# DLRM tower on one core: low parts in quarters between the one-hots, four lookups ahead of the second pair, transposes moved later

## The chip, the cores and the metric

One core of one Trainium2 chip runs the whole program. The metric is the device time in microseconds of one launch. Engines are named TensorE (PE), VectorE (DVE), ScalarE (ACT), GpSimd (POOL) and SyncE (SP).

## The reference

The batch has 2048 samples. Each has 26 ids, one into each of 26 tables of 128-wide fp32 rows, and a dense vector of 128 values. Eleven or twelve of the tables have only 1000 rows.

```python
e = stack([tbl_f[ids[:, f]] for f in range(26)], axis=1)   # (2048, 26, 128)
sd = einsum('bfd,bd->bf', e, dense)
pairs = einsum('bfd,bgd->bfg', e, e)[:, iu, ju]            # 325 pairs above the diagonal
z = concatenate([dense, sd, pairs], axis=1)
h = concatenate([z, dense], axis=1)                        # (2048, 607)
h = maximum(h @ W_top1 + b_top1, 0)                        # 512
h = maximum(h @ W_top2 + b_top2, 0)                        # 256
y = h @ W_top3
```

## The kernel before

The batch is cut into eight chunks of 256 samples, worked on in four pairs. The features of both chunks of a pair are collected in `feat`, transposed (128 values on the partitions). There are two ways into it.

**Lookups (l).** A small table is read by a matmul with one-hot columns. The table stays in SBUF as 125 partitions by 8 rows of 128, split into two parts that TensorE takes at its faster fp32r rate: a high part made by ScalarE (`split_hi`, step s) and a low part, the rest, made by VectorE (`split_lo`). ScalarE shifts the ids (`shift_ids`, i and j), VectorE makes the one-hots in four parts of two operations (`make_part`), three parts being held at a time (`PLACES`). TensorE's `lookup` takes each part with 4 matmuls, 16 in all, into one of two halves of `oh_ps`, and ScalarE copies the 512 columns to `feat` (`looked_up_to_feat`, c). The first pair has 12 lookups, the later ones 11; the tables are split during the first pair, their raw copies lying in eight buffers that later serve for other things.

**Gathers (r, q).** GpSimd gathers the rows of the other tables by indirect DMA, four DMAs for one unit, into a ring of six units. TensorE turns a unit with four transposes (`transposes`), ScalarE copies it out (`transposed_to_feat`). A q step turns a unit of the pair before. A unit's gathers wait for the transposes of the unit six before it.

**The rest.** `dot_products` (e for the pair's first chunk, d for the second, eight steps of 64 matmuls each) makes all pair products, which ScalarE and VectorE copy out and SP stores to DRAM and loads back in another layout (`store_products`, `make_z`). Layer 1 has four steps (k0 to k3, o0 to o3, m0 to m3) into `mlp_ps`, ScalarE adds the bias and cuts at zero; step 4 is layer 2; VectorE ends with `layer3`. Letters k, o and m mean chunks n-3, n-2 and n-1, with n the first chunk of the running pair.

The order of the steps is written out by hand in one list for each pair and one for the tail (`FIRST` to `TAIL`). TensorE and ScalarE both walk through these lists, each taking its own part of a step; VectorE and SP have loops of their own. Lines that the steps touch: `split_hi` L377, `shift_ids` L382, `transposed_to_feat` L391, `looked_up_to_feat` L399, `split_lo` L453, `make_part` L462, transposes L522, lookups L538, dot products L556, layer 1 L574, layer 2 L583, gathers L367, store of products L279, load of z L292 and L295.

A copy of a lookup may overwrite `feat` only when the dots of the pair before are done, and the dots need all copies of their chunk:

```python
if j:
    act.wait_ge(dots_done, 2 * j * GUNITS)          # looked_up_to_feat
...
if v == 0:                                          # dot_products
    pe.wait_ge(transposed_out, unit_no(n // 2, UNITS if n % 2 else ALONE + (n > 0)))
    pe.wait_ge(looked_up_out, looked(n // 2 + 1))
```

## Time and profile before

| what | value |
|---|---|
| median of 3 runs (lowest, highest) | 361.55 us (360.44, 361.7) |
| the profiled execution, its time | 359.05 us |
| its span, first to last instruction | 357.1 us |
| TensorE matmuls | 335.2 us busy, 94% |
| VectorE | 206.6 us, 58% |
| ScalarE | 204.0 us, 57% |
| GpSimd | 241.8 us, 68% |
| gathers, L367 | 236 DMAs, 1023 ns each |

The span leaves out what lies around the program, about 2 us. The profile is of one execution, so its durations are compared with its own time, and differences are then carried over to the median. Busy shares are means over stages with different limits; the rows further down are from single stages.

### The profile page before, as it was taken

Reading aid. Unit: us, or ns where it says so; the run is one execution under the profiler, and the core shown is the slowest. Engines: PE = TensorE matmul, PEld = TensorE weight load, DVE = VectorE, ACT = ScalarE, POOL = GpSimd, SP = SyncE. Lnnn points to the kernel's source line nnn. Section 1 sums busy time; section 2 is a strip of 40 time slices with the busy share of each in tenths; the row PEclk is TensorE's granted clock in tenths of the full one; section 3 lists DMA queues with packets and bytes.
Section 4 is the critical chain, followed back from the end, with each engine's and each line's share of the span. In section 5 each row is a group of like instructions: output and inputs, shape, how many; then the busy total and the mean of one; then the engine's idle time right before and its main releaser. Section 6 shows DMA issues by size and latency. Waiting matters only on the chain.

```text
span 357.1 us, 8260 instructions
## 1 busy us (share of the span) xinstructions
PE 335.2 (94%) x3388; PEld 286.4 (80%) x3388; DVE 206.6 (58%) x486; ACT 204.0 (57%) x267; POOL 241.8 (68%) x242
## 2 busy tenths in 40 slices
PE   0799999697999999999999999999999999999996
PEld 0677777586988888888998888898898888898885
DVE  0889898565328874628328886527427787145111
ACT  3378897484736575763663664872572666664111
POOL 6777777777777777777777777777777777720000
PEclk9999999999999999999999999999999999999999
DMA  6999729536355225254247243246236321124400
GB/s 154 241 261 250 194 61 269 148 93 164 76 143 138 65 69 132 55 127 124 53 108 183 75 105 84 68 95 155 59 83 177 100 64 48 51 51 121 113 24 1
DMA packets 46342, 40.93 MB, mean 115 GB/s; under 512 B 29039, under 2 KB 40423, under 8 KB 46306
## 3 DMA queue, kind: packets, MB, share of 16 engines
q1 hardware_dynamic: 38754, 24.94, 27.4%
q0 software_dynamic: 7552, 15.48, 17.3%
q8 instruction: 27, 0.44, 0.5%
q14 instruction: 9, 0.07, 0.1%
HBM read 34.64 MB, written 5.76 MB: 113 GB/s over the span
## 4 chain that ended last, share of the span: by engine, by line
PE 77%; POOL 8%; DMA 5%; issue 4%; DVE 3%; SPq 2%; ACT 1%; DVEq 0%
PE oh_ps L538 34%; PE dot_ps L556 15%; PE mlp_ps L574 15%; POOL rows L367 8%; PE mlp_ps L583 7%; PE tr_ps L522 7%; DMA rows<-tbl_dram,idx_sb 3%; DVE onehot L462 2%; DMA b_sb<-b_top_dram 2%; ACT feat L391 1%; DMA idx_sb<-idx_dram 0%; SPq L320 0%; SPq L316 0%; SPq L319 0%; DVE h L481 0%
## 5 line engine op out<-in xcount | busy, mean ns | idle before, releaser
L367 POOL DMA_INDIRECT rows<-tbl_dram,idx_sb x236 | 241.3, 1023 | 73.3 <-issue 70.7
L462 DVE TENSOR_SCALAR onehot<-ids_bc 125x512 fp32r<-125x512 int16 x360 | 142.4, 448 | 33.2 <-PE oh_ps L538 19.1
L538 PE MATMUL oh_ps<-onehot,table_hi 125*128 125x512 f32 x360 | 115.5, 402 | 12.0 <-DVE onehot L462 11.9
L538 PE MATMUL oh_ps<-onehot,table_lo 125*128 125x512 f32 x360 | 111.7, 392 | 0.0
L399 ACT ACTIVATE feat<-oh_ps 128x512 f32<-128x512 f32 x45 | 54.7, 1217 | 62.8 <-PE oh_ps L538 61.7
L391 ACT ACTIVATE feat<-tr_ps 128x512 f32<-128x512 f32 x59 | 73.0, 1241 | 26.3 <-PE tr_ps L522 25.8
L538 PEld LDWEIGHTS oh_ps<-onehot,table_hi 125*128 125x128 f32 x360 | 65.6, 190 | 24.4 <-issue 12.8
L538 PEld LDWEIGHTS oh_ps<-onehot,table_lo 125*128 125x128 f32 x360 | 68.1, 189 | 14.8
L556 PE MATMUL dot_ps<-feat 128*54 128x52 f32 x2048 | 57.8, 214 | 5.7 <-ACT feat L391 1.8
L556 PEld LDWEIGHTS dot_ps<-feat 128*54 128x54 f32 x2048 | 54.5, 130 | 10.1 <-issue 6.1
L471 DVE COPY dots<-dot_ps 54x416 f32<-54x416 f32 x56 | 33.2, 594 | 36.2 <-PE dot_ps L556 34.9
L574 PE MATMUL mlp_ps<-zt,w_sb 117*128 117x256 f32 x192 | 44.4, 380 | 0.0
L478 DVE TENSOR_TENSOR h<-mlp_ps,b_sb 128x256 f32<-128x256 f32 x16 | 6.8, 425 | 60.6 <-PE mlp_ps L583 60.6
L406 ACT ACTIVATE dots<-dot_ps 54x416 f32<-54x416 f32 x56 | 29.1, 522 | 18.3 <-PE dot_ps L556 15.6
L574 PEld LDWEIGHTS mlp_ps<-zt,w_sb 117*128 117x128 f32 x192 | 35.2, 190 | 4.3
L522 PE MATMUL tr_ps<-ident,rows 128*128 128x128 f32 x236 | 36.0, 275 | 1.2 <-DMA rows<-tbl_dram,idx_sb 1.2
L522 PEld LDWEIGHTS tr_ps<-ident,rows 128*128 128x128 f32 x236 | 28.1, 140 | 8.9 <-DMA rows<-tbl_dram,idx_sb 2.9
L382 ACT ACTIVATE ids_bc<-ids_bc,row_f 128x512 int16<-128x512 int16 x45 | 30.9, 701 | 3.6 <-DMA ids_bc<-ids_t_dram 3.6
L413 ACT ACTIVATE h<-mlp_ps,b_sb 128x256 f32<-128x256 f32 x32 | 15.0, 468 | 28.7 <-PE mlp_ps L574 28.7
L583 PE MATMUL mlp_ps<-w_sb,h 128*128 128x256 f32 x128 | 28.9, 379 | 0.0
L583 PEld LDWEIGHTS mlp_ps<-w_sb,h 128*128 128x128 f32 x128 | 24.1, 190 | 3.1
L574 PE MATMUL mlp_ps<-feat,w_sb 117*128 117x256 f32 (+1 forms) x64 | 14.2, 379 | 0.0
(24 smaller groups left out, 65.4 us busy)
## 6 DMA issues: line engine op xcount, KB each, us to landing
ids_bc<-ids_t_dram SPq DMA_DIRECT2D x45, 128.0 KB, 3.9
dots_scratch<-dots SPq DMA_DIRECT2D x28, 175.5 KB
rows<-tbl_dram,idx_sb POOLq DMA_INDIRECT x236
dots<-tbl_dram SPq DMA_DIRECT2D x6, 480.0 KB
w_sb<-tbl_dram SPq DMA_DIRECT2D x3, 480.0 KB
zt<-dots_scratch SPq DMA_DIRECT2D x12, 117.0 KB
dense_sb<-dense_f_dram SPq DMA_DIRECT2D x8, 128.0 KB, 2.6
zt<-tbl_dram SPq DMA_DIRECT2D x2, 480.0 KB
```

Source lines behind the costliest of these rows:

```text
L367: nc.gpsimd.indirect_dma_start(rows[:, i % RING, k, t, :], None, tables[f], bass.IndirectOffsetOnAxis(ap=idx_sb[:, j % 2, x:x + 1], axis=0 ...
L382: nc.scalar.activation(ids, ids, ACT.Identity, bias=row_f[:, 0:1]).then_inc(ids_shifted, 1)
L391: nc.scalar.activation(unit_view(u), tr_ps[:, i % 2], ACT.Copy).then_inc(transposed_out, 1)
L399: nc.scalar.activation(both, oh_ps[:, m % 2, :].rearrange("p (c b) -> p c b", c=2), ACT.Copy).then_inc(looked_up_out, 1)
L406: nc.scalar.activation(*dot_copy(n, v, 0), ACT.Copy).then_inc(dots_out_act, 1)
L462: last = nc.vector.tensor_scalar(onehot_part(m, part)[:, c, :], ids_bc[0:TP, m % IDSLOTS, :], float(part * PROWS + c), None, ALU.is_equal)
L471: nc.vector.tensor_copy(*dot_copy(n, v, 1)).then_inc(dots_out_dve, 1)
L522: last = nc.tensor.transpose(tr_ps[:, i % 2, k, t * P:(t + 1) * P], rows[:, i % RING, k, t, :], ident[:])
L538: last = nc.tensor.matmul(oh_ps[:, m % 2, :], table[0:TP, u, row * D:(row + 1) * D], onehot_part(m, part)[:, c, :], start=(table is table_ ...
L556: last = nc.tensor.matmul(dot_ps[dot_rows(t), v % 2, gi * PACK * NJ:(gi + 1) * PACK * NJ], batches.rearrange("p q f -> p (q f)"), batches[ ...
L574: last = nc.tensor.matmul(mlp_ps[:, x % 2, 0:CH], w1_sb[0:m, c, x * P:(x + 1) * P], z_of(n)[0:m, c, :], start=(c == 0), stop=(c == ZC))
L583: last = nc.tensor.matmul(mlp_ps[:, t, 0:N2], h1[:, c, t * P:(t + 1) * P], w2_sb[:, c, :], start=(c == 0), stop=(c == N1 // P - 1))
```

## The change

Parts, as the diff shows them:

- The low part of each table is made in four pieces, each right before the one-hots of the same quarter, and TensorE's lookups of the first pair wait for their own piece.
- The first table is loaded in two halves of columns and its high part made in two halves (steps a and b). Its ids are loaded by ScalarE's queue. The ids come from DRAM already repeated for all 128 partitions.
- TensorE starts with 24 transposes of the identity into `mlp_ps`.
- The sum of two blocks of W_top1 moves on VectorE from before the first pair's dots to behind those of chunk 0.
- In the second pair four lookups stand before the dots of chunk 1 instead of two. The third and fourth (`EXTRA`) write to `mlp_ps`, and layer 1 of chunk 0 waits for their copies.
- The transposes of pairs 1 to 3 stand later in the lists. One or two units of a pair are turned in the next list.
- In the tail, layer 1's last step and layer 2 of chunk 5 go before the dots of chunk 7. Two of the four stores of chunk 7's products are issued by ScalarE.

New semaphores and a helper that numbers the units without changing a number are left out here.

```diff
@@ -54,22 +54,28 @@
...
-FIRST = ("i0 s0 i1 s1 l0 c0 i2 s2 l1 c1 i3 s3 r0 l2 c2 i4 s4 r1 l3 c3 i5 s5 r2 l4 c4 s6 i6 r3 l5 c5 s7 i7 r4 "
-         "l6 c6 s8 i8 r5 l7 c7 s9 i9 r6 f l8 c8 s10 i10 l9 c9 s11 i11 r8 l10 c10 r9 j0 l11 c11 e0 e1 e2 e3 r10 j1 "
+EXTRA = (LOOKUPS[0] + 2, LOOKUPS[0] + 3)
+HALF = RPP * D // 2
+WARM = 24
...
+FIRST = ("i0 a0 b0 i1 s1 l0 c0 i2 s2 l1 c1 i3 s3 r0 l2 c2 i4 s4 r1 l3 c3 i5 s5 r2 l4 c4 s6 i6 r3 l5 c5 s7 i7 r4 "
+         "l6 c6 s8 i8 r5 l7 c7 s9 i9 r6 f l8 c8 s10 i10 l9 c9 s11 i11 r8 l10 c10 j0 l11 c11 r9 e0 e1 e2 e3 r10 j1 "
-SECOND = ("l0 q12 l1 q13 q14 d0 d1 d2 d3 d4 d5 d6 c0 d7 c1 o0 r0 o1 o2 r1 o3 r2 o4 "
-          "l2 c2 r3 i6 l3 c3 r4 i7 l4 c4 r5 i8 l5 c5 i9 l6 c6 r6 i10 l7 c7 r7 f l8 c8 r8 l9 c9 r9 l10 c10 r10 "
-          "j0 m0 g m1 e0 e1 r11 e2 e3 e4 e5 e6 e7 r12 m2 j1 m3 r13 j2 j3 m4 r14 j4 j5")
-LEAD = "l0 l1 r0 o0 o1 r1 d0 d1 d2 d3 d4 d5 d6 c0 d7 c1 r2 o2 r3 o3 o4 r4 "
-THIRD = (LEAD + "l2 c2 l3 c3 r5 i6 l4 c4 r6 i7 l5 c5 i8 r7 f l6 c6 i9 l7 c7 r8 i10 l8 c8 r9 l9 c9 l10 c10 r10 "
-         "j0 m0 g m1 r11 e0 e1 e2 e3 r12 e4 e5 e6 e7 r13 m2 j1 m3 r14 j2 j3 m4 j4 j5")
-LAST = (LEAD + "l2 c2 l3 c3 r5 i6 l4 c4 r6 i7 l5 c5 i8 r7 f l6 c6 i9 l7 c7 r8 i10 l8 c8 r9 l9 c9 r10 g l10 c10 r11 "
-        "m0 m1 r12 e0 e1 e2 e3 r13 e4 e5 e6 e7 r14")
-TAIL = "k2 d0 d1 d2 d3 d4 d5 d6 d7 k3 k4 o0 o1 o2 o3 o4 m0 m1 m2 m3 m4"
+SECOND = ("l0 q12 l1 q13 l2 l3 q14 d0 d1 d2 d3 d4 d5 d6 c0 d7 c1 c2 c3 r0 o0 o1 o2 r1 o3 r2 o4 i6 "
+          "l4 c4 r3 i7 l5 c5 r4 i8 l6 c6 r5 l7 c7 i9 l8 c8 r6 i10 f l9 c9 r7 l10 c10 r8 "
+          "j0 m0 g m1 e0 e1 e2 e3 r9 e4 e5 e6 e7 r10 m2 j1 m3 j2 r11 m4 j3 r12 j4 j5")
+THIRD = ("l0 l1 q13 o0 o1 q14 d0 d1 d2 d3 d4 d5 d6 c0 d7 c1 r0 o2 o3 r1 o4 r2 "
+         "l2 c2 r3 i6 l3 c3 i7 l4 c4 r4 i8 l5 c5 r5 l6 c6 i9 r6 l7 c7 i10 f l8 c8 r7 l9 c9 r8 l10 c10 r9 "
+         "j0 m0 g m1 e0 e1 r10 e2 e3 e4 e5 e6 e7 r11 m2 j1 r12 m3 j2 j3 m4 r13 j4 j5")
+LAST = ("l0 l1 q14 o0 o1 r0 d0 d1 d2 d3 d4 d5 d6 c0 d7 c1 r1 o2 o3 r2 o4 r3 "
+        "l2 c2 l3 c3 r4 i6 l4 c4 r5 i7 l5 c5 i8 r6 l6 c6 i9 r7 f l7 c7 i10 l8 c8 r8 l9 c9 r9 g l10 c10 r10 "
+        "m0 m1 e0 e1 e2 e3 r11 e4 e5 e6 e7 r12")
+TAIL = "k2 k3 q13 k4 q14 d0 d1 d2 d3 d4 d5 d6 d7 o0 o1 o2 o3 o4 m0 m1 m2 m3 m4"
...
+        def lookup_out(m):
+            if m in EXTRA:
+                return mlp_ps[:, EXTRA.index(m), :]
+            return oh_ps[:, m % 2, :]
...
+        def store_quarter(engine, n, q):
+            products = dots_dram[n % 2, 0:NI * NJ, :].rearrange("(i j) b -> i j b", j=NJ)
+            row = TILE * (q // PACK) + NI * (q % PACK)
+            own = dots_of(n)[row:row + NI].rearrange("p (k j g) -> p k j g", k=PACK, j=NJ)
+            engine.dma_start(products[:, :, q * QS:(q + 1) * QS], own[:, q % PACK]
+                             ).then_inc(last_stored if n == NCH - 1 else dots_stored, DMA)
...
-                sp.dma_start(ids_bc[:, m % IDSLOTS, :], ids_t[m:m + 1, :].broadcast_to([P, BOTH])
-                             ).then_inc(ids_loaded[m % IDSLOTS], DMA)
+                sp.dma_start(ids_bc[:, m % IDSLOTS, :], ids_t[m]).then_inc(ids_loaded[m % IDSLOTS], DMA)
...
+            def load_first_table():
+                raw = raw_table(0)
+                src = tables[ONEHOT[0]].rearrange("(r c) d -> r (c d)", c=RPP)
+                for half in range(2):
+                    cs = slice(half * HALF, (half + 1) * HALF)
+                    loaded = table_loaded[0] if half else half_loaded
+                    sp.dma_start(raw[0:120, cs], src[0:120, cs]).then_inc(loaded, DMA)
+                    sp.dma_start(raw[120:TP, cs], src[120:TP, cs]).then_inc(loaded, DMA)
...
-                    sp.wait_ge(lo_made, u - RAWS + 1)
+                    sp.wait_ge(lo_made, PARTS * (u - RAWS + 1))
...
-                products = dots_dram[n % 2, 0:NI * NJ, :].rearrange("(i j) b -> i j b", j=NJ)
-                for q in range(Q):
-                    row = TILE * (q // PACK) + NI * (q % PACK)
-                    own = dots_of(n)[row:row + NI].rearrange("p (k j g) -> p k j g", k=PACK, j=NJ)
-                    sp.dma_start(products[:, :, q * QS:(q + 1) * QS], own[:, q % PACK]).then_inc(dots_stored, DMA)
+                for q in range(Q if n < NCH - 1 else Q // 2):
+                    store_quarter(sp, n, q)
...
-                sp.wait_ge(dots_stored, Q * DMA * (n + 1))
+                if n == NCH - 1:
+                    sp.wait_ge(last_stored, Q * DMA)
+                else:
+                    sp.wait_ge(dots_stored, Q * DMA * (n + 1))
...
-            for u in range(IDSLOTS):
+            load_first_table()
+            for u in range(1, IDSLOTS):
...
-            sp.wait_ge(lo_made, RAWS)
+            sp.wait_ge(lo_made, PARTS * RAWS)
...
-                    for u in range(NO - 2, NO):
+                    for u in range(NO - 2, LOOKUPS[j]):
...
+            def split_first_hi(half):
+                cs = slice(half * HALF, (half + 1) * HALF)
+                act.wait_ge(table_loaded[0] if half else half_loaded, 2 * DMA)
+                nc.scalar.activation(table_hi[0:TP, 0, cs], raw_table(0)[0:TP, cs], ACT.Copy
+                                     ).then_inc(hi_made if half else half_hi_made, 1)
...
-                nc.scalar.activation(both, oh_ps[:, m % 2, :].rearrange("p (c b) -> p c b", c=2), ACT.Copy
+                nc.scalar.activation(both, lookup_out(m).rearrange("p (c b) -> p c b", c=2), ACT.Copy
...
+            act.dma_start(ids_bc[:, 0, :], ids_t[0]).then_inc(ids_loaded[0], DMA)
...
+                    if kind in "ab":
+                        split_first_hi("ab".index(kind))
...
+                    if kind == "d" and n == NCH and x == GUNITS - 1:
+                        act.wait_ge(dots_out_act, GUNITS * NCH)
+                        act.wait_ge(dots_out_dve, GUNITS * NCH)
+                        for q in range(Q // 2, Q):
+                            store_quarter(act, NCH - 1, q)
...
-            def split_lo(u):
-                dve.wait_ge(hi_made, u + 1)
-                nc.vector.tensor_tensor(table_lo[0:TP, u, :], raw_table(u)[0:TP],
-                                        table_hi[0:TP, u, :].bitcast(fp32), ALU.subtract).then_inc(lo_made, 1)
+            def split_lo(u, part):
+                if u:
+                    dve.wait_ge(hi_made, u + 1)
+                else:
+                    dve.wait_ge(half_hi_made if part < PARTS // 2 else hi_made, 1)
+                cs = slice(part * PROWS * D, (part + 1) * PROWS * D)
+                nc.vector.tensor_tensor(table_lo[0:TP, u, cs], raw_table(u)[0:TP, cs],
+                                        table_hi[0:TP, u, cs].bitcast(fp32), ALU.subtract).then_inc(lo_made, 1)
...
-                split_lo(u)
+                    split_lo(u, part)
-            dve.wait_ge(weights_loaded, WEIGHT_DMAS * DMA)
-            nc.vector.tensor_tensor(w1_sb[:, ZC, :], w1_sb[:, ZC, :], w1_dense2, ALU.add).then_inc(w1_summed, 1)
...
+                lead = PARTS * (4 if j == 1 else 2)
-                    for i in range(PLACES, 2 * PARTS + PLACES):
+                    for i in range(PLACES, lead + PLACES):
...
-                    for i in range(2 * PARTS + PLACES, NO * PARTS):
+                    for i in range(lead + PLACES, LOOKUPS[j] * PARTS):
...
-                if 0 < j < NPAIR - 1:
+                if j == 0:
+                    dve.wait_ge(weights_loaded, WEIGHT_DMAS * DMA)
+                    nc.vector.tensor_tensor(w1_sb[:, ZC, :], w1_sb[:, ZC, :], w1_dense2, ALU.add
+                                            ).then_inc(w1_summed, 1)
+                elif j < NPAIR - 1:
+            layer3(NCH - 3)
-            for n in range(NCH - 3, NCH):
+            for n in range(NCH - 2, NCH):
...
-                if j == 0:
+                if m == 0:
+                    pe.wait_ge(half_hi_made, 1)
+                elif j == 0:
-                    pe.wait_ge(lo_made, u + 1)
-                if m >= 2:
-                    pe.wait_ge(looked_up_out, m - 1)
+                if m in EXTRA:
+                    pe.wait_ge(warmed, 1)
+                elif m >= 2:
+                    pe.wait_ge(looked_up_out, m - 1 - 2 * (m - 2 in EXTRA))
+                    if m == 0 and part == PARTS // 2:
+                        pe.wait_ge(hi_made, 1)
+                    if j == 0:
+                        pe.wait_ge(lo_made, PARTS * u + part + 1)
...
-                            last = nc.tensor.matmul(oh_ps[:, m % 2, :], table[0:TP, u, row * D:(row + 1) * D],
+                            last = nc.tensor.matmul(lookup_out(m), table[0:TP, u, row * D:(row + 1) * D],
...
-                    pe.wait_ge(transposed_out, unit_no(n // 2, UNITS if n % 2 else ALONE + (n > 0)))
+                    pe.wait_ge(transposed_out, unit_no(n // 2, UNITS if n % 2 else ALONE + has_odd(n // 2)))
...
+                        pe.wait_ge(looked_up_out, EXTRA[-1] + 1)
...
+            pe.wait_ge(ident_made, 1)
+            for i in range(WARM):
+                last = nc.tensor.transpose(mlp_ps[:, i % 2, 0:P], ident[:], ident[:])
+            last.then_inc(warmed, 1)
...
+    looked_up = np.repeat(looked_up[:, None], P, 1)
```

## Rows read from the trace of the kernel before

**Rows 1.** Stretch, length, busy us of PE, PEld, DVE, ACT, POOL, clock, DMA share, GB/s.
```profile
4.50:43.00 38.50, 30.43 (x136) 24.29 (x137) 31.10 (x69) 25.55 (x28) 30.27 (x28) 1.00 0.98 244
...
11.00:13.90 2.90, 2.89 (x7) 2.32 (x8) 2.07 (x7) 1.06 (x1) 2.04 (x3) 1.00 1.01 232
...
161.10:318.30 157.20, 157.20 (x1659) 135.59 (x1658) 92.70 (x224) 91.19 (x120) 118.98 (x118) 1.00 0.37 94
```

**Rows 2.** Timeline of TensorE: start, us, what, idle before and releaser.
```profile
11.01 1.19 PE L538 MATMUL oh_ps<-onehot,table_hi 125*128 125x512 f32 x2 [11.01 <-DVE onehot L462]
...
37.94 0.66 PE L522 MATMUL tr_ps<-ident,rows 128*128 128x128 f32 x4 [0.33 <-DMA rows<-tbl_dram,idx_sb]
...
42.60 0.66 PE L522 MATMUL tr_ps<-ident,rows 128*128 128x128 f32 x4 [0.35 <-DMA rows<-tbl_dram,idx_sb]
...
65.05 1.16 PE L556 MATMUL dot_ps<-feat 128*54 128x52 f32 x38 [1.32 <-issue]
...
68.63 1.57 PE L556 MATMUL dot_ps<-feat 128*54 128x52 f32 x55 [1.77 <-DVE dots L471]
...
86.01 1.20 PE L556 MATMUL dot_ps<-feat 128*54 128x52 f32 x39 [1.84 <-ACT feat L391]
...
160.69 0.66 PE L522 MATMUL tr_ps<-ident,rows 128*128 128x128 f32 x4 [0.25 <-DMA rows<-tbl_dram,idx_sb]
```

**Rows 3.** Timeline of GpSimd: the gather before 42.60, and the last.
```profile
35.39 1.13 POOL L367 DMA_INDIRECT rows<-tbl_dram,idx_sb  x1 [0.30 <-issue]
...
314.80 0.94 POOL L367 DMA_INDIRECT rows<-tbl_dram,idx_sb  x1 [0.30 <-issue]
```

**Rows 4.** Timeline of TensorE in the third pair: three transpose groups.
```profile
187.84 0.60 PE L522 MATMUL tr_ps<-ident,rows 128*128 128x128 f32 x4
...
195.59 0.60 PE L522 MATMUL tr_ps<-ident,rows 128*128 128x128 f32 x4
...
199.69 0.49 PE L522 MATMUL tr_ps<-ident,rows 128*128 128x128 f32 x3
```

**Rows 5.** Timeline of ScalarE at the start.
```profile
5.80 0.72 ACT L382 ACTIVATE ids_bc<-ids_bc,row_f 128x512 int16<-128x512 int16 x1 [3.57 <-DMA ids_bc<-ids_t_dram]
...
7.88 1.06 ACT L377 ACTIVATE table_hi<-dots 125x1024 fp32r<-125x1024 f32 x1 [1.35 <-DMA dots<-tbl_dram]
```

**Rows 6.** Timeline of VectorE: a low part, one-hots, and a 256-element operation.
```profile
53.24 1.22 DVE L453 TENSOR_TENSOR table_lo<-dots,table_hi 125x1024 fp32r<-125x1024 f32 x1
...
54.38 2.87 DVE L462 TENSOR_SCALAR onehot<-ids_bc 125x512 fp32r<-125x512 int16 x8
...
334.06 0.42 DVE L481 SCALAR_TENSOR_TENSOR h<-h,w_sb 128x256 f32<-128x256 f32 x1
```

**Rows 7.** Timeline of TensorE and ScalarE behind the dots of chunk 1.
```profile
93.12 1.13 PE L574 MATMUL mlp_ps<-zt,w_sb 117*128 117x256 f32 x4
...
94.72 1.16 ACT L399 ACTIVATE feat<-oh_ps 128x512 f32<-128x512 f32 x1
...
95.65 0.44 ACT L413 ACTIVATE h<-mlp_ps,b_sb 128x256 f32<-128x256 f32 x1
```

**Rows 8.** Timeline before the third list's first dots (TensorE, ScalarE).
```profile
172.36 0.60 PE L522 MATMUL tr_ps<-ident,rows 128*128 128x128 f32 x4
...
173.00 1.21 ACT L391 ACTIVATE feat<-tr_ps 128x512 f32<-128x512 f32 x1
```

**Rows 9.** Timeline of TensorE and SP behind the last dots.
```profile
327.89 1.35 PE L574 MATMUL mlp_ps<-zt,w_sb 117*128 117x256 f32 x5
...
329.02 4.76 SPq L279 DMA_DIRECT2D dots_scratch<-feat  x4
...
338.81 0.48 SPq L295 DMA_DIRECT2D feat<-dots_scratch  x1
```

**Rows 10.** The chain that ended last: layer 2 and layer 1.
```profile
340.26 3.45 PE mlp_ps L583 x16
...
343.71 6.92 PE mlp_ps L574 x32
```

More of the change, by code:

```diff
@@ L86, in looked, with has_odd @@
     return sum(LOOKUPS[:j])
+def has_odd(j):
+    return LOOKUPS[j] == NO
 def unit_no(j, u):
-    return UNITS * j - (j > 0) + u - (j == 0 and u > ALONE)
+    return UNITS * j - sum(not has_odd(i) for i in range(j)) + u - (not has_odd(j) and u > ALONE)
 def pair(row):
@@ L178, in dlrm_tower @@
         ident_made = sem("ident_made")
+        warmed = sem("warmed")
+        half_loaded = sem("half_loaded")
+        half_hi_made = sem("half_hi_made")
         hi_made = sem("hi_made")
@@ L190, in dlrm_tower @@
         dots_stored = sem("dots_stored")
+        last_stored = sem("last_stored")
         z_loaded = [sem(f"z_loaded{p}") for p in range(2)]
@@ L355, in _ @@
             for j, u in itertools.product(range(NPAIR), range(UNITS)):
-                if j == 0 and u == ALONE:
+                if u == ALONE and not has_odd(j):
                     continue
```

## Prediction

> **What bounds the kernel now.** I read the stretches first, then what TensorE waited for, then the queues that feed it. From 161.10 to 318.30 us TensorE is busy for all 157.20 us [rows 1]. There reordering has nothing to win: every microsecond that TensorE newly idles is added to the end. What it idles is elsewhere [rows 2]: it starts at 11.01 us; at 37.94 and 42.60 a group of transposes waits for gathered rows; at 65.05 the first dot products wait (1.32) for ScalarE's copy of the last lookup; at 68.63 (1.77) for VectorE, which is held by the weights; at 86.01 (1.84) for the copy of the last transposes; at 160.69 (0.25) for rows.
>
> Two queues run beside it and are nearly as long. GpSimd issues gathers back to back until 314.80 [rows 3], and TensorE turns their rows last thing before the tail; if it got there much earlier in the same order, it would wait. And from 4.50 to 43.00 us the DMA engines are 0.98 busy [rows 1]: the gather issued at 35.39 [rows 3] is in SBUF 7.2 us later, when TensorE's wait at 42.60 ends.
>
> **Pitches.** From the start of one transpose group to the next with one lookup between is 199.69-195.59 = 4.10, with two lookups 195.59-187.84 = 7.75 [rows 4]. So a lookup is 3.65 us of TensorE and a transpose group 0.45; a lookup's part is 0.91. All counts of lookups, transposes, dot products and layers stay the same, so I sum only what TensorE waits more or less.
>
> **The start.** The ids come by ScalarE's queue, the first table in halves, the high part in halves, low part and one-hots by quarters. Before: ids shifted at 5.80, the table whole at 7.88, then 1.06 for the high part [rows 5] and 1.14 for the low part [rows 6], one-hots, first matmul at 11.01 [rows 2]. The first half table lands between the ids (5.80) and the whole table (7.88); I take 6.8. Then half a high part 0.55, a low piece 0.34, two one-hots 0.72: first matmul near 8.5, 2.5 us earlier. The 24 warming transposes lie in idle time. Seven matmuls took 2.9 us up to 13.90 (0.41 each) against 0.228 later, a sixteenth of the lookup [rows 1, 4]; that is the 1.2 GHz level at first, and warming may save 1.3 us more. The price of the pieces: a low part took 54.38-53.24 = 1.14; a whole one lasts 1.22, so 0.08 of each operation lies under the next. A two-input operation on 256 elements lasts 0.42, at the same overlap 0.34, and four of them 1.36; 0.42 each if they don't overlap. Eight one-hots take 2.87 [rows 6], 0.36 each. One quarter is 0.34+0.72 = 1.06 us, a table 4.24 where TensorE needs 4.10 with a transpose group: VectorE now sets the pace of the first pair by a hair.
>
> But this gain is not carried on. The groups at 37.94 and 42.60 keep their place in the order (after the lookups 5 and 6 of the first pair), their gathers are issued when GpSimd comes to them, and they come in through engines that are full with the same twelve tables and ids [rows 1, 3]. At VectorE's pace, 24 quarters from 7.35 and a last part of 0.91, the sixth lookup would be over at 33.7, near 35 with table 1 late; TensorE then waits some 3 us at 37.94. I take 42.60 as fixed. From it, at TensorE's pace, the last lookup ends at 43.05 + 5 x 3.65 + 2 x 0.45 = 62.2; at VectorE's, the fourth quarter of the running table at 44.65, 16 quarters at 1.06, 0.91 for the last part: 62.5, and a little for high parts that come late, 62.7. The group r9 that stood before the last lookup now stands behind it, inside the wait for ScalarE's copy. The copy needs 1.19 and two handovers of 0.26 together, 1.45 [rows 7, 8]: dots at 64.15 instead of 65.05. **Term: -0.9** (bounds: -3 if rows land earlier, +0.25 if a piece costs 0.42).
>
> **The w1 sum behind the dots of chunk 0.** VectorE no longer stands in front of the weights; its three next parts are done at about 63.9, before the first dots end. The wait of 1.77 before 68.63 [rows 2] goes: **-1.8**. The sum itself (0.69) then lies before the fourth part of the next table, whose place TensorE frees only later; nothing waits.
>
> **Four lookups lead.** q13 goes in front of two lookups and only q14 is left before d0. Before, two copies of transposed units stood in the wait of 1.84 before 86.01 [rows 2]. With one group it is 0.64 from its start to ScalarE's and 1.21 for the copy [rows 8], 1.92 with the handover, of which TensorE's row covers 0.60: 1.32 idle. **-0.5**.
>
> The two extra lookups write into mlp_ps. o0 therefore waits for the copy c3. c0 can't start before all of d7 is done (it overwrites feat). Before: layer 1 follows the dots at once at 93.12, while ScalarE copies c0, its share of d7, then c1 at 94.72, and takes up the next step at 95.65 [rows 7]. Now c2 and c3 follow: 95.65, 0.93 later 96.58, done 1.19 later at 97.8. TensorE has r0 (0.45) and nothing else in that time: 97.8-93.12-0.45, **+4.25**. I look for cover and find none: o1, o2 and the layer 2 are behind o0, l4 behind them. Bounds: 3.8 if copies go closer, 4.7 if r0 counts for nothing.
>
> **Rows turned later.** The wait of 0.25 before 160.69 [rows 2] goes: **-0.3**. GpSimd is not held back: a unit's gathers wait for the group six units earlier, which now comes 4 to 12 us later than before, while before it stood 15 us or more clear (its next gather always followed 0.30 after the last, as in [rows 3]). SP's load_idx(3) now waits for q14 of pair 1, 8 us later; behind it stands the store of chunk 3, due later still. In the third list q14 stands right before d0, which needs its copy. Before, the group in that place was not yet needed and TensorE did not idle behind it. Now it idles the same 1.32 as above: **+1.3**, or 1.0 to 1.6. In the last list o0 and o1 cover q14: 0. In the tail q14 again stands right before d0: **+1.3**.
>
> **The tail.** d0..d7 now come after layer 2 of chunk 5, so only chunk 6's layers (6.92 and 3.45 [rows 10], 10.4) cover the way of chunk 7's products. Before: d7 ends at 327.89, four stores take 4.76 to issue, the last z load starts to issue at 338.81 [rows 9], and if it lands as quickly as the page has it for the small dense loads (2.6, an estimate), z is there 13.5 us after d7. With two stores on each of two queues 2.4 less: 11.1, **+0.7** (0 to +3.1).
>
> **Sum.** -0.9-1.8-0.5-0.3 = -3.5; +4.25+1.3+1.3+0.7 = +7.55; together +4.05 us on the profiled span of 357.1 (time 359.05). On the median of the runs, 361.55, that is 365.6, 1.1% slower. What a measurement can tell from nothing is about 0.5%, 1.8 us.
>
> **Rivals.** (a) The clock falls in a new gap. The longest gap in full work was 1.84 us [rows 2] and the matmuls behind it kept their pitch; the new one is 4.25 us, the one at 37.94 about 3. If it falls once behind c3, the price is the 1.3 us of the first matmuls: 366.9. [...]
>
> (b) The split store doesn't shorten the way: +2.4 more, 368.0. Nothing here shows a store issued by ScalarE.
>
> (c) The gathers of the first 43 us land early (ids from separate rows, other packets), so the start passes on, at VectorE's pace: from 7.35, 48 quarters of 1.06 and 0.91: 59.2, dots at 60.6, 3.5 us better: 362.1, no change that can be told. Against it stands the 0.98 [rows 1].
>
> (d) The gap at o0 doesn't arise, since ScalarE's copies slip in earlier: 361.3. Against it the wait on dots_done, which is unchanged.
>
> (e) The other side: the start runs at TensorE's own pace throughout. From 8.5, 12 x 3.65 + 8 x 0.45 gives 55.9, dots at 57.4, 6.75 better: 358.8, faster. It needs the gathers of 37.94 and 42.60 some 6 us earlier and quarters under 1.02 us; it decides where the first dots come at 58.3 or before.
>
> **How the numbers follow.** Forecast 0.50, (a) 0.10, (b) 0.12, (c) 0.12, (d) 0.06, (e) 0.10. Forecast, (a) and (b) are slower: 0.72; (c) and (d) the same: 0.18; (e) faster: 0.10. The range reaches down to between (c) and (d), 361.5, and up to (b) with a bit of (a), 368.8. The forecast's own terms make it 363.8 to 367.3.
>
> **What the profile after would show.** First matmul near 8.5 and at the 0.228 pitch; a wait of about 3 us for rows at 38 and again a short one near 42.6; first dots near 64, the next two following without a gap; a gap of about 4 us between d7 and o0 near 98, ended by ScalarE's copy out of mlp_ps; gaps of 1.3 us before d0 of the third list and the tail; under 1 us before m0. The prediction is wrong if the first dots come before 62 us, or if layer 1 follows d7 of chunk 1 within 2 us.

## The result, and the profile after

The changed kernel takes 368.45 us (median of four runs, 367.25 to 369.5); the kernel before took 361.62 beside it. The ratio is 1.0191 (95% interval 1.0148 to 1.0234): 1.9% slower, where the prediction had 365.6 and 1.1%. The profiled execution has a span of 367.1 us (time 368.9), 10.0 more than that of before; by the medians it is 6.9, because the profiled execution of before lay 2.5 us under its median and that of the changed kernel 0.45 above. The clock has a part in that: the profiled execution of before kept it throughout, and most of its others did not (w1_again, below).

What TensorE waited for in the changed kernel: engine, tile and line <- releaser, then microseconds in total, how many times, the longest.

```profile
PE mlp_ps L645 <- ACT feat L443: 4.3, 1, 4.3
PE dot_ps L626 <- ACT feat L435: 3.8, 3, 1.3
PE tr_ps L584 <- DMA rows<-tbl_dram,idx_sb: 2.9, 2, 2.0
PE mlp_ps L645 <- DMA feat<-dots_scratch: 2.2, 1, 2.2
PE oh_ps L608 <- DVE onehot L519: 1.8, 2, 1.3
```

The first line is the gap before layer 1, the second the three groups turned right before the dots, the fourth z of chunk 7. Their places, from TensorE's timeline of the changed kernel (they answer to [rows 2]):

```profile
6.20 0.70 PE L608 MATMUL oh_ps<-onehot,table_hi 125*128 125x512 f32 x2 [0.50 <-DVE onehot L519]
25.45 0.66 PE L584 MATMUL tr_ps<-ident,rows 128*128 128x128 f32 x4 [0.88 <-DMA rows<-tbl_dram,idx_sb]
31.75 1.12 PE L584 MATMUL tr_ps<-ident,rows 128*128 128x128 f32 x4 [2.00 <-DMA rows<-tbl_dram,idx_sb]
63.51 3.59 PE L626 MATMUL dot_ps<-feat 128*54 128x52 f32 x128 [0.88 <-issue]
102.18 7.69 PE L645 MATMUL mlp_ps<-zt,w_sb 117*128 117x256 f32 x24 [4.26 <-ACT feat L443]
176.51 3.60 PE L626 MATMUL dot_ps<-feat 128*54 128x52 f32 x128 [1.27 <-ACT feat L435]
331.48 7.18 PE L626 MATMUL dot_ps<-feat 128*54 128x52 f32 x256 [1.27 <-ACT feat L435]
351.73 8.87 PE L645 MATMUL mlp_ps<-feat,w_sb 117*128 117x256 f32 x32 [2.17 <-DMA feat<-dots_scratch]
```

The line at 63.51 carries 128 matmuls without a break (a step of dots is 32 matmuls in the trace, not 64, so these are four steps): the 1.77 that stood in the middle of them [rows 2] is gone. Who fills the gap before 102.18 is seen on ScalarE:

```profile
97.42 1.18 ACT L443 ACTIVATE feat<-oh_ps 128x512 f32<-128x512 f32 x1 [1.10 <-issue]
98.38 0.57 ACT L450 ACTIVATE dots<-dot_ps 54x416 f32<-54x416 f32 x1
98.85 1.16 ACT L443 ACTIVATE feat<-oh_ps 128x512 f32<-128x512 f32 x1
99.78 2.26 ACT L443 ACTIVATE feat<-mlp_ps 128x512 f32<-128x512 f32 x2
101.80 1.24 ACT L435 ACTIVATE feat<-tr_ps 128x512 f32<-128x512 f32 x1
```

c0, ScalarE's share of d7, c1, then c2 and c3: layer 1 starts when c3 is done. That is the predicted mechanism. What it did not hold is in the windows of the changed kernel (columns: PE, PEld, DVE, ACT, POOL busy with instructions, then PEclk, DMA share, GB/s):

```profile
31.00:37.00 6.00, 5.25 (x18) 4.41 (x19) 2.48 (x7) 2.61 (x3) 4.48 (x6) 0.72 1.00 240
97.30:102.10 4.80, 0.61 (x5) 0.38 (x4) 0.59 (x1) 4.67 (x6) 3.78 (x4) 0.78 0.38 91
102.10:108.00 5.90, 5.82 (x17) 4.75 (x18) 0.00 (x0) 1.42 (x2) 4.46 (x5) 0.60 0.79 208
352.00:354.00 2.00, 2.00 (x7) 1.66 (x7) 0.00 (x0) 0.00 (x0) 0.00 (x0) 0.63 0.00 0
354.00:356.00 2.00, 2.00 (x6) 1.56 (x6) 0.00 (x0) 0.47 (x1) 0.00 (x0) 0.51 0.00 0
356.00:358.00 2.00, 2.00 (x11) 1.76 (x10) 0.00 (x0) 0.47 (x1) 0.00 (x0) 1.00 0.00 0
```

PEclk is the mean granted clock. 0.51 is the level of 1.2 GHz, 1.00 that of 2.4. It fell three times, behind the waits of 2.00, 4.26 and 2.17 us. From 354 to 356 TensorE gets through 6 matmuls, from 356 to 358 through 11.

### The profile page after: what moved, and what is told of

It is laid out like the page before. It is cut to its first block, busy times and chain, and to the rows that moved or that the text cites. A ratio compares the mean times of both kernels' runs of the same rounds, so it can differ in the third digit from the quotient of the medians.

```text
span 367.1 us, 8385 instructions
## 1 busy us (share of the span) xinstructions
PE 345.7 (94%) x3412; PEld 291.9 (80%) x3412; DVE 206.8 (56%) x522; ACT 206.0 (56%) x268; POOL 239.6 (65%) x242
## 4 chain that ended last, share of the span: by engine, by line
PE 83%; DMA 5%; POOL 4%; ACT 3%; issue 2%; SPq 1%; DVE 0%; ACTq 0%; DVEq 0%
PE oh_ps L608 38%; PE dot_ps L626 15%; PE mlp_ps L645 14%; PE tr_ps L584 7%; PE mlp_ps L654 7%; POOL rows L404 4%; DMA rows<-tbl_dram,idx_sb 2%; PE mlp_ps L608 2%; DMA dots_scratch<-feat 2%; ACT feat L435 1%; ACT feat L443 1%; DMA feat<-dots_scratch 1%; SPq L328 1%; DMA idx_sb<-idx_dram 1%; ACTq L264 0%
## 5 line engine op out<-in xcount | busy, mean ns | idle before, releaser
L608 PE MATMUL oh_ps<-onehot,table_hi 125*128 125x512 f32 x344 | 111.4, 405 | 1.8 <-DVE onehot L519 1.8
L608 PE MATMUL oh_ps<-onehot,table_lo 125*128 125x512 f32 x344 | 106.8, 392 | 0.0
L435 ACT ACTIVATE feat<-tr_ps 128x512 f32<-128x512 f32 x59 | 72.8, 1234 | 34.1 <-PE tr_ps L584 33.6
L443 ACT ACTIVATE feat<-oh_ps 128x512 f32<-128x512 f32 x43 | 52.3, 1216 | 58.4 <-PE oh_ps L608 56.6
L608 PEld LDWEIGHTS oh_ps<-onehot,table_lo 125*128 125x128 f32 x344 | 65.0, 189 | 14.3
L608 PEld LDWEIGHTS oh_ps<-onehot,table_hi 125*128 125x128 f32 x344 | 61.5, 190 | 16.0 <-issue 5.8
L645 PE MATMUL mlp_ps<-zt,w_sb 117*128 117x256 f32 x192 | 46.0, 393 | 4.3 <-ACT feat L443 4.3
L645 PEld LDWEIGHTS mlp_ps<-zt,w_sb 117*128 117x128 f32 x192 | 37.0, 198 | 9.6 <-issue 4.5
L645 PE MATMUL mlp_ps<-feat,w_sb 117*128 117x256 f32 (+1 forms) x64 | 16.3, 415 | 2.2 <-DMA feat<-dots_scratch 2.2
```

What stands on the lines that cost most here:

```text
L435: nc.scalar.activation(unit_view(u), tr_ps[:, i % 2], ACT.Copy).then_inc(transposed_out, 1)
L443: nc.scalar.activation(both, lookup_out(m).rearrange("p (c b) -> p c b", c=2), ACT.Copy).then_inc(looked_up_out, 1)
L608: last = nc.tensor.matmul(lookup_out(m), table[0:TP, u, row * D:(row + 1) * D], onehot_part(m, part)[:, c, :], start=(table is table_hi an ...
L645: last = nc.tensor.matmul(mlp_ps[:, x % 2, 0:CH], w1_sb[0:m, c, x * P:(x + 1) * P], z_of(n)[0:m, c, :], start=(c == 0), stop=(c == ZC))
```

## The experiments

Four kernels ran first, then four more. On both chips that these two sets met, every engine stood still now and then for up to some 10 us, in the kernel before as well (489.2 and 491.4 us). Whole times there can't tell 2 us apart, so of those eight runs I read single rows between the standstills. Four kernels were run again where the kernel before took 361 to 362 us; their names end in "again", and what is said of whole times rests on them.

**two_leads.** Back to two leading lookups, q13 and q14 both in front of the dots:

```diff
-EXTRA = (LOOKUPS[0] + 2, LOOKUPS[0] + 3)
+EXTRA = ()
...
-SECOND = ("l0 q12 l1 q13 l2 l3 q14 d0 ... c0 d7 c1 c2 c3 r0 o0 o1 o2 r1 o3 r2 o4 i6 "
+SECOND = ("l0 q12 l1 q13 q14 d0 ... c0 d7 c1 r0 o0 o1 o2 r1 o3 r2 o4 l2 c2 l3 c3 i6 "
...
-                lead = PARTS * (4 if j == 1 else 2)
+                lead = PARTS * 2
```

> The changed kernel with two lookups ahead of the second pair's dots instead of four; none writes to mlp_ps. My theory (the wait of 4.26 us before layer 1 of chunk 0 plus about 2.2 us of half clock behind it are added to the end in full, and the wait for q14's copy before the dots grows back from 1.27 to about 1.8): 6 us less than the changed kernel, about 362.5. Rival (TensorE, earlier by 6 us, now runs into the rows of the gathers or into VectorE later on): at most 3 us less, 365.5 or above, with new waits for rows in the second or third list.

Ratio to before 1.0248 (1.0079 to 1.0416), which tells nothing of 4 us. The rows do: r0 at 140.84, layer 1 at 141.34 with no wait, and layer 2 at 149.33, 8.0 later, where the changed kernel has 102.18 and 112.31, 10.1. Without c2 and c3 ahead of layer 1 there is neither gap nor half clock (1.00 from 140.8 to 149.4). How much of the expected 6 us this is worth in whole time, no run shows.

**warm_gap, warm_again.** Dummy transposes in the gap, everything else as changed:

```diff
+                        pe.wait_ge(dots_out_act, 2 * GUNITS)
+                        pe.wait_ge(dots_out_dve, 2 * GUNITS)
+                        for i in range(WARM):
+                            nc.tensor.transpose(dot_ps[:, i % 2, 0:P], ident[:], ident[:])
                         pe.wait_ge(looked_up_out, EXTRA[-1] + 1)
```

> The changed kernel with 24 transposes of the identity into dot_ps inside the gap before layer 1 of chunk 0, so that TensorE is not idle there; their result is not used. Theory (the clock's fall is a cost of its own, 2.2 us, beside the gap): the gap's end stays at about 102, the matmuls behind it keep the full pitch, the granted clock from 97 to 108 us stays 1.00, and the time is 2.2 us less, 366.2. Rival (the slow pitch behind the gap comes from ScalarE or the loads, not from the clock): unchanged 368.4.

> The kernel of the run 'warm_gap' once more (24 dummy transposes in the gap before o0). Theory: the gap's end stays where it was, the granted clock does not fall behind it, o0 to the place of l4 takes 11.2 us instead of 13.4, and the end comes 2.2 us earlier: span 364.9, ratio to before 1.013 where the changed kernel has 1.019. Rival: the 2.2 us come back as waits later in the list, span 367.

warm_gap: ratio 1.0255 (1.0141 to 1.0369), undecided; from o0 (146.95) to l4 (158.12) 11.17 us. warm_again: 365.77 us, ratio 1.0129 (1.0099 to 1.0158), span 365.3. Its timeline:

```profile
99.82 2.81 PE L641 MATMUL dot_ps<-ident 128*128 128x128 f32 x24 [1.29 <-ACT dots L450]
102.77 5.46 PE L649 MATMUL mlp_ps<-zt,w_sb 117*128 117x256 f32 x24
113.94 0.82 PE L608 MATMUL oh_ps<-onehot,table_hi 125*128 125x512 f32 x2
```

The granted clock from 99.8 to 108 is 1.00. The same 24 layer-1 matmuls last 5.46 here and 7.69 in the changed kernel, and o0 to l4 is 113.94-102.77 = 11.17 against 115.58-102.18 = 13.40. Layer 1 starts no earlier behind the dots than before: the work in the gap is useless, and still 2.2 us come back. So the gap of 4.26 cost 6.5 in all. By the medians it is 2.7 (368.45 against 365.77), though the intervals of the two ratios just touch; the rows decide. Nothing gave it back later: the tail's dots come at 329.70 against 331.48, although the first dots were 1.06 later (64.57).

**q14_early.** q14 beside q13, in the third list and the tail (the 1.27 waits):

```diff
-THIRD = ("l0 l1 q13 o0 o1 q14 d0 ...
+THIRD = ("l0 l1 q13 q14 o0 o1 d0 ...
...
-TAIL = "k2 k3 q13 k4 q14 d0 ...
+TAIL = "k2 k3 q13 q14 k4 d0 ...
```

> The changed kernel with q14 moved ahead of o0 in the third list and ahead of k4 in the tail, so that other work covers its copy. Theory: both waits of 1.27 us before the dots go, 2.5 us less, 365.9. Rival (the rows of q14 land too late for the earlier place, GpSimd is the bound): waits for rows appear in their place and the time moves by less than 1 us.

Ratio 1.0226 (1.0088 to 1.0364), undecided. Of three waits for L435 one is left, 1.27 at 140.63 in the second list; the gap before layer 1 is 4.26 as before, and o0 to l4 takes 13.85: the half clock comes with the gap here too (0.50 from 156.9 to 162). No wait for rows takes the place of the two, but a run stretched by standstills says little about rows; best_again, further down, says more.

**stores_on_sp.** All four stores of chunk 7's products by SyncE, as in the kernel before:

```diff
-                for q in range(Q if n < NCH - 1 else Q // 2):
+                for q in range(Q):
...
-                    if kind == "d" and n == NCH and x == GUNITS - 1:
-                        act.wait_ge(dots_out_act, GUNITS * NCH)
-                        act.wait_ge(dots_out_dve, GUNITS * NCH)
-                        for q in range(Q // 2, Q):
-                            store_quarter(act, NCH - 1, q)
```

> The changed kernel with all four stores of chunk 7's products issued by SP. Theory (the stores' own transfer, not their issue, sets when the z loads may start; they started 7.38 us after the first store against 7.46 before): the wait before layer 1 of chunk 7 stays within 0.5 us of 2.17 and the time within 0.6 us of 368.45. Rival (the split saves the 2.4 us of issue): the wait grows to about 4.5 us and the time to 370.8.

Its time, 495.12 us, tells nothing; its tail lies between standstills:

```profile
459.74 7.19 PE L640 MATMUL mlp_ps<-feat,w_sb 117*128 117x256 f32 x32
466.76 3.61 PE L649 MATMUL mlp_ps<-w_sb,h 128*128 128x256 f32 x16
472.64 8.87 PE L640 MATMUL mlp_ps<-feat,w_sb 117*128 117x256 f32 x32 [2.27 <-DMA feat<-dots_scratch]
```

The wait is 2.27, with the split 2.17. But the split also stretches the work that covers it, so the way from the end of the dots to the last layer 1 is the better measure: 472.64-459.74 = 12.90 without the split, 351.73-338.59 = 13.14 with it. The split gains nothing, where 2.4 had been reckoned.

**w1_only, w1_again.** The kernel before, with the w1 sum behind chunk 0's dots alone:

```diff
-            dve.wait_ge(weights_loaded, WEIGHT_DMAS * DMA)
-            nc.vector.tensor_tensor(w1_sb[:, ZC, :], w1_sb[:, ZC, :], w1_dense2, ALU.add).then_inc(w1_summed, 1)
...
-                if 0 < j < NPAIR - 1:
+                if j == 0:
+                    dve.wait_ge(weights_loaded, WEIGHT_DMAS * DMA)
+                    nc.vector.tensor_tensor(w1_sb[:, ZC, :], w1_sb[:, ZC, :], w1_dense2, ALU.add
+                                            ).then_inc(w1_summed, 1)
+                elif j < NPAIR - 1:
```

> The kernel before with one edit: the sum of the two parts of w1 stands behind chunk 0's dot products on VectorE instead of behind the last quarter of the first pair. Theory (the prediction's second term): VectorE no longer holds the second dot products, the wait of 1.77 us at 68.63 goes, and nothing takes its place: chunk 0's last dot product and all behind it come 1.8 us earlier, the span is 355.3 against 357.1, ratio 0.995. Rival: the 1.8 us come back as waits for gathered rows in the long lists, since GpSimd issues gathers back to back: span within 0.5 us of before, the wait at 160.69 (0.25) grown to about 2.

> The kernel of the run 'w1_only' once more, since that run's kernels stood still too often to tell 2 us. Theory: the wait of 1.77 us before chunk 0's second dot products goes, nothing takes its place, span 355.3 against 357.1, ratio 0.995. Rival: it comes back as waits for gathered rows in the long lists, the one of 0.25 at 160.69 grown to about 2, ratio 1.000.

w1_only gave 0.9956 (0.9833 to 1.0078), undecided. w1_again: 359.0 us, ratio 0.9967 (0.9936 to 0.9998), span 356.5. The interval holds the 0.995 of the theory and ends just short of the rival's 1.000, so the times don't decide between them. TensorE's timeline speaks for the rival:

```profile
65.05 3.60 PE L558 MATMUL dot_ps<-feat 128*54 128x52 f32 x128 [1.32 <-issue]
82.63 0.66 PE L524 MATMUL tr_ps<-ident,rows 128*128 128x128 f32 x4 [0.67 <-DMA rows<-tbl_dram,idx_sb]
84.55 7.18 PE L558 MATMUL dot_ps<-feat 128*54 128x52 f32 x256 [1.27 <-ACT feat L391]
140.74 0.66 PE L524 MATMUL tr_ps<-ident,rows 128*128 128x128 f32 x4 [1.06 <-DMA rows<-tbl_dram,idx_sb]
144.79 1.41 PE L558 MATMUL dot_ps<-feat 128*54 128x52 f32 x48
```

The wait of 1.77 is gone, but two waits for gathered rows (0.67 and 1.06) come up, and the dots at 144.79 come to the hundredth where the kernel before has them. GpSimd issues its last gather at 314.77 there, at 314.80 before [rows 3]. In the order of the kernel before, TensorE runs up against the gathers. The medians differ by 1.9 us all the same (359.0 against 360.88), and the mean granted clock separates the two. Of 13 executions of the kernel before, measured beside w1_again, seven have a clock of 0.995 (median 361.5 us) and six one of 0.999 or 1.000 (median 359.7); beside best_again all seven have 0.995 or less. Of ten executions of w1_again nine have 1.000, with a median of 359.0. So at the same clock some 0.7 us is left, and the rest goes with falls of the clock that come less often. Which wait lets it fall in the kernel before, no kept trace shows; the 1.77 at 68.63 and the 1.84 at 86.01, here gone and 1.27, are the longest in full work [rows 2].

**start_old, start_again.** The changed kernel with the start as before, but for the ids, which still come already repeated for all partitions (first matmul at 9.69, in the kernel before at 11.01 [rows 2]):

```diff
-FIRST = ("i0 a0 b0 i1 s1 l0 ...
+FIRST = ("i0 s0 i1 s1 l0 ...
...
-            load_first_table()
-            for u in range(1, IDSLOTS):
+            for u in range(IDSLOTS):
...
-            act.dma_start(ids_bc[:, 0, :], ids_t[0]).then_inc(ids_loaded[0], DMA)
...
+                split_lo(u)
                 for part in range(PARTS):
-                    split_lo(u, part)
...
-            for i in range(WARM):
-                last = nc.tensor.transpose(mlp_ps[:, i % 2, 0:P], ident[:], ident[:])
```

> The changed kernel with the start wholly as before: the first table whole, ids by SyncE, no warming transposes, the low parts whole. Theory (the gathered rows pin the start): the first dot products come 1.1 us later than in the changed kernel (63.51 there, 65.05 before, the copy of r9 no longer in front of it), and the end the same 1.1 later, 1.0 to 1.6: span 368.2, ratio to before 1.022. Rival (the start's gain of 4.8 us at the first matmul passes on wholly): the end comes 4 to 5 us later, span 371.5.

> The kernel of the run 'start_old' once more (the changed kernel with the start wholly as before), for the same reason. Theory: the start's gain reaches the first dot products by 1.1 us (65.05 - 0.45 for the copy of the last row group is 64.6 against 63.51) and the end by the same, span 368.2, ratio 1.022. Since in the records the granted clock halves behind the wait of 2.0 us for rows at 31.75, a second theory: with the old start TensorE waits there less, the clock stays up, and the old start is within 0.5 us of the new one. Rival: the gain of 4.8 us at the first matmul passes on wholly, span 371.5.

start_old gave 1.0042 (0.9965 to 1.0119), undecided. start_again: 369.38 us, ratio 1.023 (1.0207 to 1.0253), span 369.4:

```profile
9.69 1.19 PE L595 MATMUL oh_ps<-onehot,table_hi 125*128 125x512 f32 x2 [9.69 <-DVE onehot L512]
39.39 0.66 PE L577 MATMUL tr_ps<-ident,rows 128*128 128x128 f32 x4 [2.28 <-DMA rows<-tbl_dram,idx_sb]
65.87 3.59 PE L613 MATMUL dot_ps<-feat 128*54 128x52 f32 x128 [0.88 <-issue]
355.74 7.19 PE L632 MATMUL mlp_ps<-feat,w_sb 117*128 117x256 f32 x32 [2.33 <-DMA feat<-dots_scratch]
```

The new start is 3.49 us ahead at the first matmul (9.69 against 6.20) and 2.36 at the first dots; in two other executions with the new start (best_again and warm_again) the first dots come at 63.91 and 64.57, 1.96 and 1.30 ahead. So rows take part of it, as in the theory, but in this pair less than I had reckoned. At the end nothing is settled: the profiled execution of start_again is its slowest (371.3 us), its last layer 1 begins 4.01 later than in the changed kernel, and 1.7 of that comes back because its clock stays up at the end. By the medians the start is worth 0.9, and the intervals of the two ratios overlap (1.0148 to 1.0234 and 1.0207 to 1.0253). The second theory, that the old start waits less for rows, failed: it waits 2.28 where the new one waits 2.00. And the clock stays up here behind 2.28 and behind 2.33: from 38 to 44 and from 354 to 358 it is 1.00.

**whole_low.** Only the first table's low part in pieces:

```diff
+                if u and part:
+                    return
-                cs = slice(part * PROWS * D, (part + 1) * PROWS * D)
+                cs = slice(0, RPP * D) if u else slice(part * PROWS * D, (part + 1) * PROWS * D)
...
-                                        table_hi[0:TP, u, cs].bitcast(fp32), ALU.subtract).then_inc(lo_made, 1)
+                                        table_hi[0:TP, u, cs].bitcast(fp32), ALU.subtract).then_inc(lo_made, PARTS if u else 1)
```

> The changed kernel, but only the first table has its low part made in four pieces; those of tables 1 to 11 are made whole. Theory (the pieces matter at the first table alone, since a table's lookup takes 3.65 us of TensorE and its quarters 4.24 of VectorE): the whole low parts save VectorE 4 x 0.34 - 1.14 = 0.22 us a table and the span stays within 0.5 us of the changed kernel. Rival (VectorE sets the first pair's pace by its pieces): the first dot products come 2 us earlier or more, 61.5. Second rival (a whole low part delays the first quarter of each table by 0.8 us and TensorE waits for it each time): first dot products 2 us or more later, 65.5.

Ratio 1.0054 (0.9966 to 1.0141), first dots at 89.94 among standstills, where start_old has 88.17. That decides nothing: what the pieces of tables 1 to 11 are worth stays open.

**best, best_again.** The changed kernel with its gaps filled:

```diff
-SECOND = ("l0 q12 l1 q13 l2 l3 q14 d0 ... c1 c2 c3 r0 o0 o1 o2 r1 o3 r2 o4 i6 l4 c4 r3 ...
+SECOND = ("l0 q12 l1 q13 l2 l3 q14 d0 ... c1 c2 c3 r0 l4 c4 o0 o1 o2 r1 o3 r2 o4 i6 r3 ...
...
-THIRD = ("l0 l1 q13 o0 o1 q14 d0 ...
+THIRD = ("l0 l1 q13 q14 o0 o1 d0 ...
...
-TAIL = "k2 k3 q13 k4 q14 d0 d1 d2 d3 d4 d5 d6 d7 o0 ...
+TAIL = "k2 q13 q14 k3 d0 d1 d2 d3 d4 d5 d6 d7 k4 o0 ...
```

VectorE makes the one-hots of l4 ahead of layer 1 as well, and does layer 3 of chunk 5 behind the dots of chunk 7.

> The changed kernel with its three new gaps filled: l4 and c4 of the second list stand between r0 and o0 (3.65 us of lookup in the gap of 4.26), in the third list q13 and q14 stand together ahead of o0 and o1, and in the tail they stand ahead of k3 and of the dots. Theory: the wait at o0 falls from 4.26 to 0.6 or less and TensorE's granted clock does not fall behind it (o0 to l4 cost 13.4 us with it, 11.1 without), the 1.27 us waits before d0 of the third list and the tail go: 367.1 - 3.7 - 2.3 - 2.5 = 358.6 of span if nothing else gives way, ratio to before about 1.00 (0.995 to 1.005). Rival (the gap only moves: c4 behind c3 on ScalarE makes o0 wait for the same copy): a wait of 1 us or more at o0 and a span of 361 or more, ratio 1.01. Second rival: the clock gate falls elsewhere, for the 2.0 us wait at 31.75 stays.

> The kernel of the run 'best' once more. There it stood at 0.9857 of the kernel before, but both kernels were some 35% slower than in the first measurement, with standstills of all engines of up to 10 us. Theory, where the kernel before again takes about 361 us: the first dot products near 63.5, no wait over 1 us at o0 and no half clock behind it, o0 to l4's place 11.2 us, a wait under 0.5 us before m0: 367.1 - 3.5 (gap at o0) - 2.3 (clock behind it) - 2.5 (q14 twice) - 1.7 (m0) - 1.8 (clock at the end) = 355.3 of span, ratio 0.995. Rival: the second list's other order costs what the gap gave back, and the span stays at 360 or more.

best: 482.76 us, ratio 0.9857 (0.978 to 0.9935). best_again: 356.61 us, ratio 0.9846 (0.9823 to 0.9869), span 355.1 where 355.3 was expected. It is 1.5% faster than the kernel before, with every part of the change still in it but one: layer 2 of chunk 5 (k4) is behind the dots of chunk 7 again, as in the kernel before:

```profile
32.18 0.66 PE L587 MATMUL tr_ps<-ident,rows 128*128 128x128 f32 x4 [2.23 <-DMA rows<-tbl_dram,idx_sb]
98.60 0.73 PE L611 MATMUL oh_ps<-onehot,table_hi 125*128 125x512 f32 x2 [0.74 <-ACT feat L443]
102.36 5.35 PE L648 MATMUL mlp_ps<-zt,w_sb 117*128 117x256 f32 x24
319.79 7.23 PE L629 MATMUL dot_ps<-feat 128*54 128x52 f32 x252
341.47 7.19 PE L648 MATMUL mlp_ps<-feat,w_sb 117*128 117x256 f32 x32 [0.42 <-DMA feat<-dots_scratch]
```

l4 starts after 0.74 us and covers c2 and c3; layer 1 then runs at the full clock. From r0 to r3, with the same work in between, it is 16.4 us (97.20 to 113.61), in the changed kernel 22.2 (97.26 to 119.42). Nothing waits before the dots of the third list or the tail, and behind 32.18 nothing waits for rows: that is the answer to the rival of q14_early. k4 behind the dots gives chunk 7's products 3.5 us more cover, and the last wait falls to 0.42, with the clock up behind it. The gain over the changed kernel was measured for these moves together, not for each.

## Why the prediction was right or wrong

The sign, the place of the largest gap and its size were right, and the time lies in the range, 0.35 us below its upper end and above the 367.3 that the forecast's own terms allow. It got in there by the mechanisms of two rivals that I had taken one at a time: the clock fell (a), and the split store gained nothing (b). Both together by my own prices make 369.3, outside the range; that the time still lies inside is partly luck. Term by term:

- **Start, -0.9.** Measured -1.54 at the first dots (63.51 against 65.05). The first matmul came at 6.20, not near 8.5: the ids were shifted at 3.19, and the high part of the half table, for which I had taken 6.8, began at 4.29. The warming worked: the first two matmuls last 0.70, without it 1.19 (start_again). The same start gave 63.91 in best_again and 64.57 in warm_again, so 64.15 was within the scatter. Its reason failed in part: I took the group near 42.60 as fixed. That group waited for nothing (41.62), though in warm_again it waited 0.96 (42.70). The waits came two groups earlier (25.45, 31.75), and against its own counterpart, start_again, the start brings 2.36.
- **w1 sum, -1.8, and rows, -0.3.** Both held in the changed kernel: no wait for rows behind 31.75. But they are one term, not two. In the profile of w1_again the gain of the sum alone is lost to row waits by 144.79. That the later turning is what lets it through fits the changed kernel, but no run has the later turning alone. I had costed the turning at the 0.25 us of the wait that the trace before showed.
- **Four leads, -0.5.** 1.27 where I had 1.32.
- **o0, +4.25.** 4.26. two_leads shows that c2 and c3 are the cause, best_again that one lookup in front of layer 1 covers them. I had looked for cover among o1, o2 and the layer 2 and wrote that l4 stood behind them; it could be moved.
- **q14, +1.3 twice.** 1.27 twice.
- **m0, +0.7.** 2.17, within the bound of 3.1. This is a mis-sized step: "With two stores on each of two queues 2.4 less". The way from the first store to the first z load was 336.48-329.02 = 7.46 before and is 346.75-339.37 = 7.38. The chain of the changed kernel shows why:

```profile
339.38 1.62 ACTq L264
341.00 0.03 issue
341.03 5.70 DMA dots_scratch<-feat
346.73 0.02 issue
346.75 0.77 SPq L328
```

  The issue got shorter and the landing (5.70) took what it gave. In the other three kernels with the split and without standstills this way takes 7.29 (warm_again), 8.57 (start_again) and 8.82 (best_again), in stores_on_sp 7.22. That is what the Trainium skill ("DMA: Bandwidth & Descriptors", "Issuing engines are not separate DMA queues") says, that two issuers save only issue time; stores_on_sp agrees (12.90 against 13.14 from the dots to the last layer 1). ScalarE pays as well: its two issues last 2.43, the relu of o0 comes at 341.85, and o0 to layer 2 takes 7.35 (338.59 to 345.94) instead of 6.92 [rows 10]; in start_again, where the two issues last 3.37, it takes 8.29.
- **The clock, rival (a) at 0.10 and 1.3 us.** This is the step that failed. It costs 2.2 behind o0 (shown by warm_again), and at the end 8.71 instead of 6.92, 1.8 (351.73 to 360.44; without the fall 7.02 in best_again and start_again). Two errors: a gap of 4.25 had no counterpart in the trace, and I let the kept pitch behind 1.84 us speak for it; and I priced it by seven matmuls at the start, though 24 wide ones stand behind the gap. Nor does that row show the level that I read from it: its granted clock is 1.00 [rows 1], and only the pitch of the matmuls (0.41 against 0.228) tells of a slow start. That the clock never fell in the trace before was luck of the execution, too: in most others of that kernel it did (14 of 20, beside w1_again and best_again). The Trainium skill ("TensorE: Matmul & The Clock Gate", "HAM oscillation") describes a kernel whose waits for DMA let TensorE fall back, so that the matmuls behind each wait start slow; all of this case's gaps of 4.26 agree.

Sum of the measured: -1.54-1.77-0.57-0.25 (start, w1, q14 before the second list's dots, rows) +4.26+1.27+1.27+2.17 = +4.8; clock 2.2+1.8, ScalarE's issue 0.4: 9.2 of the 10.0. Some 0.7 more lies in the second list's dots, 7.86 from 89.40 to the next transposes at 97.26, 7.11 before (86.01 to 93.12), and 7.41 to 7.50 in the other undisturbed kernels with four leads. 0.49 of it is a pause at 96.33 for which the profile names no releaser; why is open. Such pauses lie elsewhere as well: the tail's dots lasted 7.72 before and 7.11 here. So the sum closes to about half a microsecond and not to the tenth. By the medians it is 6.9, of which I had 4.05; the median of before already holds falls of the clock that its profile doesn't have.

## What to carry to other kernels

A wait on the busiest engine is priced as the gap plus the clock behind it, and here that was half as much again (4.26 and 2.2); so look for an independent unit of work to stand in the gap: a lookup there made the stretch 5.8 us shorter (22.2 to 16.4). One profiled execution can be one of those in which the clock held, so the mean clock of the other executions belongs beside it. Before a saving is counted, ask which queue runs just behind: a stall removed from TensorE alone was lost to the gathers in the profile. Splitting a store over two issuing queues is no gain where the landing, not the issue, ends the wait.

## What the runs showed of the hardware

- Near 2 us the clock's answer is not fixed. Behind waits of 1.92, 2.00, 2.17 and 2.23 us it fell (warm_again at 349.98, the changed kernel twice, best_again at 32.18, where the clock from 31 to 36 is 0.67); behind 1.73, 2.28 and 2.33 it did not (warm_again at 31.83, start_again twice). Behind 4.26 it fell in all six kernels that have this gap (changed, start_again and the four among standstills, 0.50 behind each), and cost 2.2 to 2.7: 13.40 (changed), 13.75 (start_again) and 13.85 (q14_early) for the stretch that takes 11.17 at the full clock.
- Gathered rows land up to a microsecond apart from run to run while the DMA engines are full: with one and the same start the group of transposes at 41.62 didn't wait, in warm_again it waited 0.96 and stood at 42.70, and the first dots came at 63.51, 63.91 and 64.57.
- A program on one core can run 35% slower on one chip at one time than on another, with all engines standing still for up to some 10 us. Rows between the standstills (4.26, 1.27, 11.17) then agreed to the hundredth with those of undisturbed runs, while whole times couldn't tell 2 us.
- Two stores issued by ScalarE held it for 2.43 us (changed) and 3.37 us (start_again), and the next activation began 0.04 us behind them.
